# The gate projection z moved one gap earlier in plain slots of a selective scan, with a half projection and one convolution moved beside it

## The reference, cut to what matters

```
xz = rmsnorm(layernorm(x)) @ W_in;  xs, res = split(xz)      # 1024 channels each
xs = silu(causal_conv4(xs) + conv_b)
dt_r, B, C = split(xs @ W_xp)                                # 128, 16, 16
delta = softplus(dt_r @ W_dt + b_dt)
h[t] = h[t-1] * exp(delta*A) + delta*B*xs                    # 16 states a channel
y = (sum over states of h*C + xs*D) * silu(res)
out = y @ W_out + x
```

## Time and profile before

| | us |
|---|---|
| median of 3 runs | 1585.88 (1583.93 to 1586.73) |
| profiled execution | 1580.36 |
| its span | 1578.3 |
| mean granted TensorE clock | 0.972 |

### The profile page before, as it was taken

How to read it: one execution, slowest core, us unless ns; L and a number is a source line. 1 busy time by engine, 2 the same in 40 slices (tenths; PEclk the granted TensorE clock), 3 DMA queues, 4 the chain that set the end, 5 groups by cost and what they waited for, 6 DMA issues and landing times.

```text
span 1578.3 us, 14721 instructions
## 1 busy us (share of the span) xinstructions
PE 1434.1 (91%) x4412; PEld 722.2 (46%) x4413; DVE 1314.4 (83%) x1931; ACT 744.0 (47%) x1160; POOL 1077.5 (68%) x545
## 2 busy tenths in 40 slices
PE   6678999899999799999888787999999999999997
PEld 3223444344344344444333333544445666667775
DVE  5589999999999999999999999464656868777772
ACT  4656666767656776655666665342000221211111
POOL 0299998999987999998999989150001446455453
PEclk9889999999999899999999999999999999999999
DMA  4540112510112510102410002231403788888995
GB/s 134 226 179 9 44 31 90 214 42 31 36 32 89 213 42 29 37 22 74 180 35 30 9 20 107 67 114 34 187 32 114 209 229 228 252 234 250 265 245 67
DMA packets 63822, 176.85 MB, mean 112 GB/s; under 512 B 10304, under 2 KB 15168, under 8 KB 55040
## 3 DMA queue, kind: packets, MB, share of 16 engines
q1 hardware_dynamic: 48128, 138.59, 25.4%
q0 software_dynamic: 15616, 37.32, 11.4%
HBM read 142.98 MB, written 32.85 MB: 111 GB/s over the span
## 4 chain that ended last, share of the span: by engine, by line
PE 42%; POOL 25%; DVE 19%; DMA 7%; issue 7%; ACT 1%; POOLq 0%; SPq 0%; DVEq 0%; ACTq 0%
POOL h L1368 14%; DVE h L957 10%; PE bank L1920 8%; PE bank L1569 8%; PE bank L1530 7%; DMA out<-y,slot_token 6%; DVE h L947 4%; POOL h L1355 4%; PE bank L1962 4%; PE bank L1537 4%; PE bank L1466 3%; POOL h L1373 3%; PE bank L1498 2%; PE bank L1488 2%; DVE xs L926 2%
## 5 line engine op out<-in xcount | busy, mean ns | idle before, releaser
L1368 POOL TENSOR_TENSOR h<-h,c_rep 128x2048 f32<-128x2048 f32 x128 | 578.6, 4526 | 20.0 <-DVE h L957 14.8
L1569 PE MATMUL bank<-h,ident 128*128 128x512 f32 x916 | 442.7, 627 | 73.5 <-POOL h L1368 57.8
L728 ACT ACTIVATE bank<-delta,a_neg 128x512 f32<-128x512 f32 x512 | 338.6, 684 | 151.7 <-DVE h L957 150.0
L1569 PEld LDWEIGHTS bank<-h,ident 128*128 128x128 f32 x916 | 181.9, 202 | 312.7 <-issue 219.3
L957 DVE TENSOR_TENSOR_SCAN h<-bank,state,h 128x512 f32<-128x512 f32 x256 | 306.9, 1265 | 1.3
L957 DVE TENSOR_TENSOR_SCAN h<-bank,h 128x512 f32<-128x512 f32 x256 | 291.5, 1204 | 3.7 <-ACT bank L728 2.7
L173 DVE STREAM_TRANSPOSE xT<-xg 32x256 f32<-32x256 f32 (+1 forms) x592 | 247.0, 417 | 24.6 <-DMA xg<-flat,slot_token 16.9
L947 DVE TENSOR_TENSOR h<-bank,b_rep 128x2048 f32<-128x2048 f32 (+1 forms) x105 | 228.8, 2179 | 21.6 <-ACT bank L719 18.3
L1920 PE MATMUL bank<-xT,w_ring 128*128 128x256 f32 x1024 | 227.4, 380 | 0.0
L1920 PEld LDWEIGHTS bank<-xT,w_ring 128*128 128x128 f32 x1024 | 193.8, 190 | 41.2 <-issue 16.6
L1729 POOL DMA_INDIRECT out<-y,slot_token x64 | 101.5, 1586 | 108.4 <-DMA out<-y,slot_token 63.6
(11 more groups left out here) (236 smaller groups left out, 1477.0 us busy)
## 6 DMA issues: line engine op xcount, KB each, us to landing
w_ring<-in_w SPq DMA_DIRECT2D x32, 1024.0 KB
b_rep<-bcd SPq DMA_DIRECT2D x16, 1024.0 KB, 4.8
c_rep<-bcd SPq DMA_DIRECT2D x16, 1024.0 KB, 5.0
w_ring<-in_w SPq DMA_DIRECT2D x32, 512.0 KB
w_in<-in_w_in_x SPq DMA_DIRECT2D x32, 256.0 KB, 2.6
w_res<-in_w_in_res SPq DMA_DIRECT2D x32, 256.0 KB, 2.6
xa<-in_x SPq DMA_DIRECT2D x20, 256.0 KB, 3.1
xb<-in_x SPq DMA_DIRECT2D x16, 256.0 KB, 2.7
```

Source lines behind the costliest of these rows:

```text
L728: eng.activation(da[j][:], delta[:, g % 2], ACT.Exp, scale=a_neg[:, col:col + 1])\
L1368: ins = eng.tensor_tensor(h[:, q], h[:, q], c_rep[:, Q * q:Q * q + Q, :], ALU.mult)
L1569: ins = eng.matmul(y_ps[:], c.ident[:], h[:, q, j, :], start=False, stop=(q == NQ - 1 and j == Q - 1))
```

## The change

Three moves; no instruction is added or removed. In plain slots z stands in gap 1, after the other items of that gap, and not in gap 2. The half output projection of slot 31 stands in its gap 0 and not in gap 1. On VectorE the convolution of the blocks of gap 1 stands behind the first scans of the slot. The order in which the items follow one another on TensorE, and so their banks, stays as it is.

```diff
@@ gap_items
             if g == LAST - 1:
                 gaps[3].append(("out", NSEG - 1, 0, 0))
             if g == LAST:
-                gaps[1].append(("out", NSEG - 1, 1, 0))
-            gaps[2].append(("z", (g + 1) // DC, g + 1, 0))
+                gaps[0].append(("out", NSEG - 1, 1, 0))
+            gaps[2 if leaving(g) or dense(g) else 1].append(("z", (g + 1) // DC, g + 1, 0))
             gaps[3].insert(0, ("dt", (g + 2) // DC, g + 2, 0))
@@ VectorE's loop
                 for g in range(LAST + 1):
                     s, d = divmod(g, DC)
+                    scans(g, 0)
                     front(g - 1, 1)
-                    scans(g, 0)
```

## The result

The changed kernel takes 1567.88 us (median of 5 runs, 1567.40 to 1572.41) against 1584.98 us of the kernel before beside it (5 runs, 1583.93 to 1586.73): ratio 0.9896, 95% interval [0.9882, 0.9911], 16.5 us less. In a later set of runs, beside 16 of the kernel before, it was 0.9897 [0.9866, 0.9928]. On the 1585.88 us that the prediction starts from the ratio gives 1569.4 us, against 1572.4 predicted.

A forecast was written before the change was run, and what follows sets the result against it. Bound by whichever closes last in the scan loop: VectorE's own slot work, or GpSimd with TensorE. Terms 2.1 + 4.9 + 2.97 + 3.6 = 13.6, say 13.5 us, off 1585.88 give 1572.4 us; range 1567.5 to 1580.5.

The forecast's parts named there:

- Part 1: Slots 0 to 2: z a gap sooner removes GpSimd's waits for TensorE; 2.1 us, despite a new wait at slot 3.
- Part 2: Slots 4, 5, 12, 13, 20, 21: convolution behind first scans removes VectorE's idle; 2.10 + 0.44 + 2.35 = 4.9 us.
- Part 3: Slots 6, 7, 14, 15: VectorE has no idle and GpSimd waits for it, so moving z brings nothing.
- Part 4: Slot 22: z a gap sooner removes GpSimd's whole wait, so VectorE gets du of slot 24 sooner; 2.97 us.
- Part 5: Slots 27 to 31 and the end: last scans and TensorE's last sums end earlier; half projection's move neutral; 3.6 us.
- Rival A: Dense slots: GpSimd or TensorE sets the pace, so convolution and tail savings pass only partly; 9 us, 1577 us; 20%.
- Rival B: Whole loop: the moves bring nothing, each wait taken comes back as another; 3 us left, 1583 us; 7%.
- Rival C: Six convolution slots: late convolution holds ScalarE's SiLU and dt's bank, 3 us each; 4.5 us slower, 1590 us; 5%.

The follow-up runs named there:

- e7: Kernel before with z moved a gap sooner in slots 27 to 30 alone, last half projection left in place: 1580.76 us, ratio 0.9969.
- e2: Kernel before with only the convolution of gap 1 moved behind the first scans: 1579.92 us, ratio 0.9966.
- e5: Kernel before with z moved a gap sooner in slots 0 to 2 alone: 1580.36 us, ratio 0.9963.
- e6: Kernel before with z moved a gap sooner in slot 22 alone: 1582.81 us, ratio 0.9984.
- e9: Changed kernel with the closing part's four index-table casts done by GpSimd in place of VectorE: 1573.53 us, ratio 0.9903.
- e11: Kernel before with the closing part's four index-table casts done by GpSimd in place of VectorE: 1584.41 us, ratio 0.9978.
- e8: Changed kernel with the convolution put later still, behind both halves of a slot's scans: 1578.72 us, ratio 0.9959.

## Why the prediction was right

- Part 1, 2.1 us (2.1 to 2.5): z in slots 0 to 2 gave 2.0 to 2.7 by slot 2 and, alone, 3.3 by slot 3. The wait forecast for GpSimd at slot 3's half product didn't come: TensorE now waited for VectorE's gate at slot 2's start and then ran summations 0 and 1 back to back in 7.86 us, with no pause and no 6.6 us row, and the product at 154.05 has no idle. The forecast kept the slow row (6.74 us behind a pause of 3.14) for the new order. It belongs to the pause: summation 1 of slot 2 is slow in five of the six profiles that have a pause of 3.1 to 4.1 us before it (e7 has 3.70), and in none of the eight with z moved in slots 0 to 2, where the pause is 0.2 us or none.
- Part 2, 4.9 us: e2 has 2.06 of the 2.10 in slot 4 and 1.9 of the 2.35 in slot 20; the 0.44 between was chance. GpSimd caught up as forecast, and dt had its bank in time. That is 4.0; the rest of e2's 5.0 is made of plus and minus 0.7 to 1.5 us at slots 2, 18, 22, 23 and 30, places at which the profiles of the other kernels vary as well.
- Part 3, nothing: right in the change. Slot 17 lost 1.0 us that no term had.
- Part 4, 2.97 us: alone 3.0. In the change 4.5, with the 1.5 us of small waits around slot 21 that went by themselves as TensorE was less behind. The term was read from one profile, and 1.7 of its 2.97 us are the slow summation 2 there, which e2 and e5 don't have.
- Part 5, 3.6 us: alone and in the change 3.8, 1.4 at slot 30 and 2.35 at slot 31. The 1.4 is again a slow summation of the profile before (slot 28): e2 and e6 have it without z's move. The tail is paced by VectorE, and GpSimd waits for scans (929.00 above). The half projection is neutral there, as the sum had it; it would be worth 1.2 without z's move.
- The sum: 13.6 forecast, 14.9 in the loop. The largest mis-sized term is slot 22's (1.5 too low). From the profile to the median I added 5.5 us as constant, for which the rows had no reason; the runs after lie 0.5 us from the profile (1567.41 and 1567.88), and that is more than the whole 4.5 us that the forecast was too high. "My sum takes nothing for it", said of the clock, was not so: some 3 us of parts 4 and 5 were the clock's. That the sum came so near is in part luck: it started from a profile that had these slow summations, and the second set of runs after has its median at 1572.84.
- Rival A would have given 9; in e2 2.06 of 2.10 and 1.9 of 2.35 us come through, so it falls. Rival B falls with the ratio. Rival C named the right place at half its price (1.4 us a slot at a greater lateness; it had 3) for a convolution later than the one here.

What stays open: why a closing part of one profile is 212 and of the next 219 us. That an instruction of VectorE ends only with GpSimd's products is shown by their rows; what decides who goes first is not. Holding GpSimd's second eight products until VectorE has summed its masks should take the meeting away; it wasn't run. Open too: what makes a summation behind one pause slow and not behind another as long.

## What to carry to other kernels

Filler work on the engine that two others wait for belongs in the widest gap of the loop, and the gaps are read from the follower's timeline: here 3.4 us of projection a gap sooner gave 10 us without removing an instruction. Such work right behind a wait also adds to what a slow clock after the wait costs. Work on the pacing engine that nobody needs soon goes behind the work whose inputs are already there, but count what is queued on its buffer: four scans later was free, eight cost 1.4 us a slot. Split the profile at fixed instants before comparing runs; a loop that repeats to 0.2 us was hidden in times that vary by 8.

## What the runs showed that I had not expected

**An instruction of VectorE held over eight of GpSimd.** VectorE's first cast of the closing part in the first profile after, and in the one of the change run again (its GpSimd row second):

```profile
1033.77 0.68 DVE L1049 CAST iota<-iota_i 128x128 f32<-128x128 int32 x1
1034.38 1.31 DVE L1049 CAST iota_h<-iota_i 128x128 f16<-128x128 int32 x1
1035.61 1.25 DVE L1049 CAST tok<-tok_i 128x16 f32<-128x16 int32 x1
```

```profile
1031.77 9.29 DVE L1049 CAST iota<-iota_i 128x128 f32<-128x128 int32 x1
1040.98 0.21 DVE L1049 CAST iota_h<-iota_i 128x128 f16<-128x128 int32 x1
...
1031.09 9.89 POOL L1413 TENSOR_TENSOR flat_normed<-flat_normed,norm_rep 128x512 f32<-128x512 f32 x8
```

The cast ends when GpSimd's eight products (1.23 us each, back to back) end; in the other profile the casts got in between them, the second and third in about one product's time each. VectorE's reductions, its MAX8 and the products with a bank operand were not held in the profiles that I read. The chain of waits shows it as the path (start, duration, what), where in the first profile the same stretch is TensorE's:

```profile
1031.17 0.69 DVE prob L1046
1031.86 9.20 DVE iota L1049
1041.06 0.14 DVE iota_h L1049
```

The Trainium skill, "SBUF — State Buffer", section SBUF: two separate sides, says that VectorE and GpSimd share a pair of ports as an exclusive lock, for VectorE's instructions in a two-port mode or with two SBUF inputs. For two SBUF inputs the trace agrees (e9: 8.82 us); in which mode the cast runs no run here shows. The page gives the lock to one instruction at a time; here VectorE was held over a row of eight.

**TensorE's low clock decides about 1 to 2 us at a time.** A summation is 3.60 us at full clock and 4.8 to 6.8 when partly at the low level, behind pauses of 1.8 to 6.7 us, but not behind each: before, at 955.14 and 962.26, pauses of 2.87 and 3.42 us are followed by 3.70. In e11 it fell on summation 2 of slot 1, ahead of z (5.40 for 3.70), and 1.7 us were lost by the gate of slot 2 and never came back (e2 has the same 5.40 at 123.31 and is 1.2 behind at slot 2). Another 2.6 went by the gate of slot 7, with summation 2 of slot 6 at 5.40 us (272.55).

```profile
122.20 5.40 PE L1570 MATMUL bank<-h,ident 128*128 128x512 f32 x8 [3.28 <-POOL h L1366]
127.43 3.60 PE L1499 MATMUL bank<-xnT,w_res 128*128 128x512 f32 x8
```

Whole times of before varied from 1579.3 to 1594.3 us in the 35 runs beside e5 to e8. How much of that is the clock and how much the closing part's 6.5 us isn't shown: in these runs time and mean granted clock go together only loosely (correlation -0.5). The three profiles with the loop of before or nearly so took 934.8, 933.1 and 939.0 us; the four with the change's loop but for the half projection 919.8, 920.1, 920.2 and 920.5. That the new order, in which fewer summations stand right behind a pause, is also the steadier one is what these few show; I did not test it by itself.
